# A decoder layer on one core: loop's end reordered, the last group's kept products added by GpSimd

## The reference

```python
x = _layernorm(x + attn(x, ...))                 # state-space block, 128 heads of 64, 8 groups
x = _layernorm(x + xattn(x, ctx, ctx, 0, mask))  # 32 query heads, 8 key heads of 16, context 128
x = _layernorm(x + ffn(x, W_gate, W_up, W_down)) # 1792 wide, silu(gate) * up
```

## Time and profile before

| | us |
|---|---|
| median of 3 runs (1641.96 to 1643.02) | 1642.07 |
| the profiled execution | 1646.22 |
| its span, first to last instruction | 1644.4 |

### The profile page before, as it was taken

One profiled execution on the slowest core, in us unless ns is written; L12 is line 12 of the kernel. 1 busy time (PEld: TensorE's weight loads), 2 busy tenths in 40 slices (PEclk: granted clock), 3 DMA queues, 4 the chain that ended last, 5 costly groups with the idle time before them and its releaser, 6 DMA issues.

```text
span 1644.4 us, 25600 instructions
## 1 busy us (share of the span) xinstructions
PE 1615.6 (98%) x9120; PEld 1274.3 (77%) x9120; DVE 1196.1 (73%) x2360; ACT 947.6 (58%) x1578; POOL 968.2 (59%) x736
## 2 busy tenths in 40 slices
PE   9999999999999999999999999999999998889998
PEld 7788888888888888888888888888888885445646
DVE  7767687767877786768686868586858688995433
ACT  6765377446745583648364837383728366994231
POOL 2977478656956694759484949495938563331000
PEclk9999999999999999999999999999999999999999
DMA  5432134212312241224131423141414173000000
GB/s 190 152 108 78 58 104 134 78 59 100 131 59 83 90 135 58 90 76 131 63 103 58 135 74 106 46 135 60 133 45 135 58 104 111 1 21 20 13 14 26
DMA packets 76547, 138.85 MB, mean 84 GB/s; under 512 B 6786, under 2 KB 13954, under 8 KB 76164
## 3 DMA queue, kind: packets, MB, share of 16 engines
q1 hardware_dynamic: 76420, 137.21, 26.3%
HBM read 134.55 MB, written 2.63 MB: 83 GB/s over the span
## 4 chain that ended last, share of the span: by engine, by line
PE 90%; DVE 7%; issue 1%; DMA 1%; ACT 0%; POOL 0%; SPq 0%; DVEq 0%; POOLq 0%; ACTq 0%
PE ps_hs L249 8%; PE ps_hs L251 8%; PE ps_hs L250 8%; PE ps_gate L250 7%; PE ps_gate L249 7%; PE ps_gate L251 7%; PE ps_y L1211 7%; PE ps_hs L1219 7%; PE ps_hs L1221 7%; PE ps_hs L1220 7%; PE ps_gate L1195 4%; PE ps_y L1503 3%; PE ps_hs L1465 3%; PE ps_dec L1465 3%; DVE pr L1043 2%; DVE conv L781 1%
## 5 line engine op out<-in xcount | busy, mean ns | idle before, releaser
L781 DVE SCALAR_TENSOR_TENSOR conv<-ps_hs,cw,conv 128x508 f32<-128x508 f32 (+2 forms) x432 | 320.2, 741 | 31.7 <-ACT conv L550 20.5
L395 POOL TENSOR_TENSOR cum_bc<-cum_bc,neg_cum 128x1024 f32<-128x1024 f32 x128 | 247.5, 1934 | 10.8 <-POOL cum_bc L385 0.3
L249 PE MATMUL ps_hs<-x_hi,w_hi 128*128 128x512 f32 x576 | 231.3, 402 | 0.0
L251 PE MATMUL ps_hs<-x_hi,w_lo 128*128 128x512 f32 x576 | 225.1, 391 | 0.0
L249 PE MATMUL ps_gate<-x_hi,w_hi 128*128 128x512 f32 x576 | 224.3, 389 | 0.0
L250 PE MATMUL ps_hs<-x_lo,w_hi 128*128 128x512 f32 x576 | 224.2, 389 | 0.0
L250 PE MATMUL ps_gate<-x_lo,w_hi 128*128 128x512 f32 x576 | 224.1, 389 | 0.0
L251 PE MATMUL ps_gate<-x_hi,w_lo 128*128 128x512 f32 x576 | 224.1, 389 | 0.0
L1219 PE MATMUL ps_hs<-wo_hi,g_hi 128*128 128x512 f32 x488 | 190.9, 391 | 0.0
L1221 PE MATMUL ps_hs<-wo_hi,g_lo 128*128 128x512 f32 x488 | 190.6, 390 | 0.0
L1220 PE MATMUL ps_hs<-wo_lo,g_hi 128*128 128x512 f32 x488 | 190.6, 390 | 0.0
(11 more groups left out here) (176 smaller groups left out, 3331.9 us busy)
## 6 DMA issues: line engine op xcount, KB each, us to landing
cum_bc<-cum_scratch SPq DMA_DIRECT2D x128, 512.0 KB, 4.1
w_raw<-w_in SPq DMA_DIRECT2D x145, 256.0 KB, 4.6
wo_raw<-w_out SPq DMA_DIRECT2D x64, 256.0 KB, 4.9
g_acc<-x_t SPq DMA_DIRECT2D x4, 512.0 KB, 6.2
acc<-x_nat SPq DMA_DIRECT2D x1, 2048.0 KB, 9.8
k_rep<-ctx_t SPq DMA_DIRECT2D x8, 256.0 KB, 12.9
out<-y_out SPq DMA_DIRECT2D x8, 256.0 KB, 2.0
wg_sb<-w_gate SPq DMA_DIRECT2D x1, 1792.0 KB, 15.7
```

The costliest lines, as they stand in the source:

```text
L249: eng.matmul(ps, whi, xhi, start=(k == 0), stop=False)
L251: return eng.matmul(ps, wlo, xhi, start=False, stop=(k == n - 1))
L395: gp.tensor_tensor(part, part, start.broadcast_to([P, 2, HB, SEQ]), ALU.add).then_inc(S["bc_ok"], 1)
L781: v.scalar_tensor_tensor(out=dst, in0=src, scalar=cw[:, at, TAPS - 1 - n:TAPS - n], in1=dst, op0=ALU.mult, op1=ALU.add).then_inc(S["tap"], 1)
```

## The change

- **Start.** Three passes over `dt`, the negation of `a_col` and the multiply by it go from VectorE to GpSimd, between `split(1)` and `split(2)`; ScalarE's L531 uses Relu instead of Identity. TensorE and SP wait for the new counts.
- **Loads.** `k_rep` is loaded from DRAM twice (to partitions 0 and 64 on); `v_raw` follows; SP waits for the two, and six DMAs copy them on inside SBUF.
- **Loop's end.** Kept products: ScalarE multiplies `g_acc` by `rstd_g` (`scale_kept`), GpSimd adds (`add_kept`), batches 0 to 4 after `k_bd` 1, 5 and 6 after 2, 7 after 3. VectorE's `second_part` waits for this; `first_part` is gone. Batch 0 alone is normed first. `LAST_PS` gives the batches other banks. TensorE does batches 0 to 2, turns the queries of batch 0, and does 3 to 7 among the first scores; VectorE's adds 3 to 7 stand in chunks 0 to 3.
- **Attention.** From batch 2 on, queries are turned into `ps_y[0]` (`Q_PS`), and ScalarE copies them ahead of its exponentials. `X2_STEPS` is two iterations earlier; `x2_high` stands ahead of the exponentials and `x2_low` between the two halves of the masked chunk. GpSimd's `powers` come in three parts (batch 1; 2 and 3; 4 to 7) and, for the second norm, at iteration 23 instead of 24.
- **Tail.** TensorE leaves its loop two iterations earlier and mixes the last turns and values with the first MLP tiles.

The diff, cut:

```diff
-X2_STEPS = (27, 29, 31, 33)
+X2_STEPS = (25, 27, 29, 31)
...
-        LAST_PS = ps_hs + ps_gate + ps_dec + ps_gate
+        LAST_PS = ps_hs + ps_dec + ps_gate + [ps_y[1], ps_y[0]]
...
+        Q_PS = (BACK_PS, BACK_PS, PV_PS)
...
-                for r in range(REP):
+                src = ctx_t.rearrange("b (c q d) t -> q d (b c) t", q=2, d=AD)[par]
+                sp.dma_start(k_rep[par * 64:par * 64 + AD, :, :, :].rearrange("p b c t -> p (b c) t"), src)\
+                    .then_inc(S["k_in"], 16)
+            sp.dma_start(v_raw[:, :, :], ctx_nat.rearrange("b t d -> t b d")).then_inc(S["v_in"], 16)
+            sp.wait_ge(S["k_in"], 16 * 2)
+            for par in range(2):
+                first = k_rep[par * 64:par * 64 + AD, :, :, :]
+                for r in range(1, REP):
                     p0 = par * 64 + r * AD
-                    src = ctx_t.rearrange("b (c q d) t -> q d (b c) t", q=2, d=AD)[par]
-                    sp.dma_start(k_rep[p0:p0 + AD, :, :, :].rearrange("p b c t -> p (b c) t"), src)\
-                        .then_inc(S["k_in"], 16)
-            sp.dma_start(v_raw[:, :, :], ctx_nat.rearrange("b t d -> t b d")).then_inc(S["v_in"], 16)
+                    sp.dma_start(k_rep[p0:p0 + AD, :, :, :], first).then_inc(S["k_in"], 16)
...
             split(1)
+            pool.wait_ge(S["a_exp"], 1)
+            gp.tensor_scalar(a_col[:, :], a_col[:, :], -1.0, None, ALU.mult).then_inc(S["dt_pool"], 1)
+            pool.wait_ge(S["dt_dve"], 2)
+            pool.wait_ge(S["dt_act"], 6)
+            gp.tensor_tensor(dt_l, dt_l, dt_u, ALU.subtract).then_inc(S["dt_pool"], 1)
+            pool.wait_ge(S["dt_pool"], 2)
+            gp.tensor_tensor(dt_v, dt_v, dt_l, ALU.add).then_inc(S["dt_pool"], 1)
+            pool.wait_ge(S["dt_pool"], 3)
+            gp.tensor_scalar(dt_v, dt_v, 100.0, 0.0, ALU.min, ALU.max).then_inc(S["dt_pool"], 1)
+            pool.wait_ge(S["dt_pool"], 4)
+            gp.tensor_tensor(dt_u, dt_v, a_col[:, 0:1].broadcast_to([P, TOK]), ALU.mult).then_inc(S["dt_pool"], 1)
...
-            def powers(stage, cols):
+            def add_kept(b):
+                pool.wait_ge(S["acc_ok"], BATCH * (GROUPS - 2) + b + 1)
+                pool.wait_ge(S["kept_sc"], b + 1)
+                gp.tensor_tensor(acc[:, b, :], acc[:, b, :], g_acc[:, b, :], ALU.add).then_inc(S["acc_ok"], 1)
...
+                if i == 1:
+                    for b in range(5):
+                        add_kept(b)
+                    powers(1, 0, slice(1, 2))
+                if i == 2:
+                    add_kept(5)
+                    add_kept(6)
                 if i == 3:
-                    powers(1, slice(2, HB))
-                if i == 7:
-                    powers(1, slice(HB, BATCH))
-                if i == 24:
-                    powers(2, slice(0, HB))
+                    add_kept(7)
+                if i == 3:
+                    powers(1, 1, slice(2, HB))
+                if i == 8:
+                    powers(1, 2, slice(HB, BATCH))
+                if i == 23:
+                    powers(2, 0, slice(0, HB))
...
-                sc.activation(dt_v[:, h * HALF:(h + 1) * HALF], ps_y[h][:, :], ACT.Identity, bias=dtb_col[:, :])\
+                sc.activation(dt_v[:, h * HALF:(h + 1) * HALF], ps_y[h][:, :], ACT.Relu, bias=dtb_col[:, :])\
...
-                sc.activation(q_t[b % 2][:, :, :].rearrange("p k s -> p (k s)"), BACK_PS[:, :], ACT.Copy,
+                sc.activation(q_t[b % 2][:, :, :].rearrange("p k s -> p (k s)"), Q_PS[min(b, 2)][:, :], ACT.Copy,
...
-            root(1, 0, slice(0, 2))
+            def scale_kept(b):
+                sc.activation(g_acc[:, b, :], g_acc[:, b, :], ACT.Copy, scale=rstd_g[:, b:b + 1])\
+                    .then_inc(S["kept_sc"], 1)
+            act.wait_ge(S["rstd_inv"], GROUPS)
+            act.wait_ge(S["gacc_ok"], BATCH * (2 * GROUPS - 1))
+            for b in range(3):
+                scale_kept(b)
+            root(1, 0, slice(0, 1))
+            sc.activation(rstd[2][:, 0:1], ones[:, 0:1], ACT.Exp).then_inc(S["exp_table"], 1)
             keep_queries(0)
-            sc.activation(rstd[2][:, 0:1], ones[:, 0:1], ACT.Exp).then_inc(S["exp_table"], 1)
+            for b in range(3, BATCH):
+                scale_kept(b)
             act.wait_ge(S["g_ok"], 2 * TILES)
             for i in range(1, CHUNKS + 3):
                 if 0 <= i - 3 < CHUNKS:
                     keep_turned(i - 3)
+                if i == 3:
+                    keep_queries(1)
+                if i % KD == 1 and 1 < i // KD + 1 < BATCH:
+                    keep_queries(i // KD + 1)
+                if i in X2_STEPS:
+                    x2_high(X2_STEPS.index(i), BACK_PS)
                 if i - 1 < CHUNKS:
                     exponentials(i - 1, 0)
-                if i % KD == 1 and i // KD + 1 < BATCH:
-                    keep_queries(i // KD + 1)
                 if i % 2 == 0 and i >= 6:
                     keep_values((i - 6) // 2)
                 if i - 1 < CHUNKS:
                     exponentials(i - 1, 1)
-                if i in X2_STEPS:
...
-            dve.wait_ge(S["dt_dve"], 2)
-            dve.wait_ge(S["dt_act"], 6)
-            v.tensor_tensor(dt_l, dt_l, dt_u, ALU.subtract).then_inc(S["dt_dve"], 1)
-            dve.wait_ge(S["dt_dve"], 3)
-            v.scalar_tensor_tensor(out=dt_v, in0=dt_v, scalar=0.0, in1=dt_l, op0=ALU.max, op1=ALU.add)\
-                .then_inc(S["dt_dve"], 1)
-            dve.wait_ge(S["dt_dve"], 4)
-            v.tensor_scalar(dt_v, dt_v, 100.0, 0.0, ALU.min, ALU.max).then_inc(S["dt_dve"], 1)
             taps(0, 0, 1)
             taps(0, 1, 0)
             taps(0, 1, 1)
-            dve.wait_ge(S["a_exp"], 1)
-            v.tensor_scalar(a_col[:, :], a_col[:, :], -1.0, None, ALU.mult).then_inc(S["dt_dve"], 1)
-            dve.wait_ge(S["dt_dve"], 6)
-            v.tensor_scalar(dt_u, dt_v, a_col[:, 0:1], None, ALU.mult).then_inc(S["dt_dve"], 1)
...
             dve.wait_ge(S["gacc_ok"], BATCH * (2 * GROUPS - 1))
             invert_group(GROUPS - 1)
-            for b in range(2):
-                first_part(b)
-                second_part(b)
-                first_stats(b)
-            variances(1, 0, first_two)
-            first_part(2)
+            second_part(0)
+            first_stats(0)
+            variances(1, 0, slice(0, 1))
+            inverses(1, 0, slice(0, 1))
+            normed(1, 0, acc[:, 0, :]).then_inc(S["x1_ok"], 1)
+            second_part(1)
             second_part(2)
-            inverses(1, 0, first_two)
-            normed(1, 0, acc[:, 0, :]).then_inc(S["x1_ok"], 1)
-            for b in range(3, 5):
-                first_part(b)
-                second_part(b)
-            normed(1, 1, acc[:, 1, :]).then_inc(S["x1_ok"], 1)
-            first_part(5)
-            second_part(5)
-            first_part(6)
-            first_part(7)
...
                     masked(i, 0)
-                    if i == 0:
-                        second_part(7)
+                    if i in X2_STEPS:
+                        x2_low(X2_STEPS.index(i), BACK_PS)
                     masked(i, 1)
-                if i + 2 < BATCH:
-                    first_stats(i + 2)
+                if i == 0:
+                    second_part(3)
+                    first_stats(1)
+                if i == 1:
+                    second_part(4)
+                    second_part(5)
+                    dve.wait_ge(S["pow1"], 1)
+                    normed(1, 1, acc[:, 1, :]).then_inc(S["x1_ok"], 1)
+                if i == 2:
+                    second_part(6)
+                    first_stats(2)
+                    first_stats(3)
+                if i == 3:
+                    second_part(7)
+                if 3 <= i < BATCH - 1:
+                    first_stats(i + 1)
                 if i % 2 == 0 and i >= 8:
                     n = (i - 8) // 2
...
-                    dve.wait_ge(S["pow1"], 1 + b // HB)
+                    dve.wait_ge(S["pow1"], 2 + b // HB)
                     normed(1, b, acc[:, b, :]).then_inc(S["x1_ok"], 1)
-                if i == 24:
+                if i == 23:
                     dve.wait_ge(S["pow2"], 1)
                 if i + 2 in X2_STEPS:
                     b = X2_STEPS.index(i + 2)
                     normed(2, b, acc[:, b, :]).then_inc(S["x2_ok"], 1)
-                if i in X2_STEPS:
-                    x2_low(X2_STEPS.index(i), BACK_PS)
             dve.wait_ge(S["kbd_ok"], CHUNKS)
...
+            last_products((4,), (0, 1))
             outputs(t, 0)
...
+            last_products((5,), (0, 1))
             outputs(t, 1)
...
+            pe.wait_ge(S["ss_part"], 1)
+            last_products((2,), range(TPH))
             pe.wait_ge(S["g_lo_ok"], 2 * t + 2)
-            pe.wait_ge(S["ss_part"], 1)
-            last_products((4, 5), range(TPH))
             def turn_queries(b):
...
-                    need(pe, S["q_sb"], b)
+                need(pe, S["q_sb"], b)
```

(47 more changed lines are left out.)

51 lines of the change are left out of this document (21 added, 30 removed).

## The result

| | us | | us |
|---|---|---|---|
| before, median of 6 | 1642.34 (1641.87 to 1644.38) | before, profiled execution | 1646.22, span 1644.4 |
| after, median of 6 | **1650.47** (1648.96 to 1652.45) | after, profiled execution | 1649.57, span 1647.7 |

The ratio after to before is 1.0036 (95% interval 1.0022 to 1.0050), some 6 us; the two medians lie 8.1 us apart, at the upper end of that interval. The forecast was 1642.8, its range ended at 1647.0, and it gave "slower" a chance of 0.22.

A forecast was written before the change was run, and what follows sets the result against it. TensorE was taken as full from 60 to 1340 us, with waits at the start and in the attention loop. Terms 2.6 - 8.6 + 3.5 + 1.8 = -0.7 us gave 1646.9 profiled, 1642.8 against the median; range 1631.5 to 1647.

The forecast's parts named there:

- part 3: Attention loop: query turns no longer wait for VectorE's attention result; 3.5 us gained, bounds 1 and 5.3.
- their cover: Attention loop: VectorE's 3.4 us a chunk was to cover GpSimd's power steps holding up k_bd; nothing counted.
- the sum: Whole kernel: 2.6 - 8.6 + 3.5 + 1.8 = -0.7 us, so 1646.9 profiled and 1642.8 against the median.
- Part 1, the start: Kernel start: passes moved from VectorE to GpSimd let the scan and causal step start earlier; 2.6 us gained, bounds 2.0 and 3.2.
- Part 2, the entry: Attention loop's entry: TensorE idles 8.5 us because the adds wait for k_rep's copies; -8.6 us, bounds +1.6 and -15.
- A: Entry, the forecast itself: copies move at 16 partitions' pace and TensorE's idle time eats the rest; 1638.5 to 1646.5, chance 0.50.
- B: Entry: copies run as fast as the weights, k_rep there by 1351 us; 1632.6 us, chance 0.28.
- C: Entry: copies of the two halves overlap in part, k_rep at 1358 us; 1637.6 us, chance 0.14.
- D: Entry: copies to partitions 32 and 96 take twice as long, k_rep at 1367.2 us; 1647.5 us, chance 0.08.
- the wait named: Attention loop: TensorE's query turns waiting for VectorE's attention result, 5.4 us in 5 places, were to stop waiting.
- the row's 5.3 us: Attention loop: ScalarE's waits for TensorE's turned probabilities, 5.3 us, taken as the upper bound of the loop's gain.
- Part 4, the tail: Attention's end: the MLP's first products start earlier, mixed with the last turns and values; 1.8 us gained, bounds 0 and 3.

The follow-up runs named there:

- e2: Kernel before with only the stage 2 power step moved from behind k_bd 24 to behind k_bd 23: ratio 1.0041 to the kernel before.
- e1: Changed kernel with the stage 2 power step of batches 0 to 3 back behind k_bd 24: ratio 1.0015 to the kernel before.
- e9: Kernel before with the start part alone (three passes and the multiply by GpSimd, Relu by ScalarE): ratio 0.9993 to the kernel before.
- e13: Kernel before with the start part, and GpSimd's next weight split waiting for VectorE's eight scans: ratio 0.9979 to the kernel before.
- e6: Changed kernel with k_rep filled by two copies of 16 partitions and two of 32, instead of six of 16: ratio 1.0017 to the kernel before.
- e12: Changed kernel with k_rep filled by two 64-partition loads from 64 consecutive DRAM rows, no copies: ratio 0.9965 to the kernel before.
- e8: Changed kernel with the query turns' wait for VectorE's attention result put back: ratio 1.0072 to the kernel before.
- e10: Changed kernel with the loop's last turns and values ahead of the MLP's first products again: ratio 1.0047 to the kernel before.
- e4: Changed kernel with k_rep filled by two 64-partition loads whose DRAM source repeats 16 rows four times, no copies: ratio 1.0164 to the kernel before.
- e14: Changed kernel with adds before k_rep's wait, power step split, two 16- and two 32-partition copies, weight split waiting for scans: 1632.76 us, ratio 0.9922 to the kernel before.

## Why the prediction was wrong

**The step that failed** is a sentence of part 3: "GpSimd's power steps hold up fewer k_bd; their cover is VectorE's 3.4 us a chunk, and I count nothing." One of them holds up k_bd 24 for longer than the cover: TensorE idles 4.5 us and comes back at half clock, 5.6 us in the trace, 6.7 alone (e2), 3.4 to 4.4 back when undone (e1). I counted how many k_bd stand behind power steps and not on what each step waits. The dependency could be read from the code: batch 3's statistics are made in VectorE's chunk 22, behind scores 22, and k_bd 24 may be made as soon as scores 22 are done; a step between k_bd 23 and 24 that needs these statistics takes away all of k_bd 24's lead.

A second step failed in the last line of the sum, "That one is 4.15 us above the median of 1642.07; against the median it is" 1642.8: by the medians it is worth 5.0 us, as much as the stall, by the ratio 2.6 (see "The sum" below).

Part 1, the start: **2.6 forecast, 2.2 in the pair of traces, 1.5 on average of twelve, 1.2 by e9's times.** GpSimd's passes were right to 0.8 us. But "the scan starts at 28.8 instead of 32.65 us" was followed by the round trip "at 39.0 instead of 42.58 us", which carried the scans' 2.63 us over to a place where GpSimd's weight split runs beside them; they took 5.55 (e13 shows it). I named the split only as something that is wanted late, not as something that disturbs.

Part 2, the entry: -8.6 forecast, **-7.8 measured**, by the way argued. k_bd 0 "starts near 1360 us": 1360.27. "Idle for some 8 us": 8.15. The copies kept the pace of 16 partitions: the first landed at 1347.8, the last at 1360.2, 2.5 us each for 2.36. This, and e6 and e12, bear A out, the forecast's own case; B, C and D fall. (D, at 1647.5, lay outside the range that was to reach it.)

Part 3, the loop: +3.5 forecast, +4.5 up to chunk 20, by the wait named (e8). The mechanism was right and the size 1 us too low: ScalarE was expected to keep 1.8 of the row's 5.3 us back, and 0.8 stayed away; no run shows whose those are.

Part 4, the tail: +1.8 forecast, +2.9 from n = 28. The MLP's first product starts at 1487.48 us, level with the earlier trace rows although chunk 31's copy is 6.6 us late, because it now stands ahead of the last turns; e10 shows 1.3 us of the gain as the order's. The forecast's bounds were "0 if the clock falls as it did, 3 if no wait is left"; the clock did not fall, and the upper bound came.

**The sum.** Without the stall these terms give a gain of 2.3 us where the forecast's sum gave a loss of 0.7: the profiled execution of after would take 1644.0. With it, it takes 1649.6, 2.7 above the forecast's 1646.9: 5.6 us of stall less 3.0 by which the other terms came out better, 1 us of it in the loop and 1.6 behind chunk 21. The forecast of the median is off by 7.7, so the other 5.0 us lie in the transfer: I took "4.15 us above the median" as a constant of the profile, and the changed kernel's profiled execution lies 0.9 below its median. The ratio, 6 us, puts this error at 2.6 us instead. The window behind the tile loop shows how executions differ, for the kernel before and then for e9:

```profile
1349.00:1359.00 10.00, 9.96 (x41) 8.20 (x42) 7.03 (x15) 2.58 (x4) 0.25 (x2) 0.66 1.26 119
```

```profile
1350.00:1356.00 6.00, 6.00 (x29) 5.03 (x29) 4.23 (x11) 1.08 (x2) 0.00 (x0) 0.73 1.28 97
```

In both, TensorE is busy throughout and its clock is at the 1.2 GHz level for a part, which costs 3.4 us before (0.34 of 10) and 1.6 in e9 (0.27 of 6). e2, built like the kernel before, has the short form too, and in both the slip is 1.6 us smaller at n = 0 than at the mask's load. So executions differ by some 1.7 us at this place. In the changed kernel the stretch costs nothing, since TensorE idles behind it anyway until the copies are there; this can be one reason why the times differ by more than the two traces. That the runs behind the median had the short stretch is not shown, and e13, whose trace has the long one (3.4 us), lies only 0.4 above its median. What the record does show is that the kernel before's own runs spread with their mean granted clock: beside e1 the fastest took 1641.40 us at 0.998 and the slowest 1648.59 at 0.994, and the profiled one, 1646.22, had 0.996. The rest I can't place.

## What to carry to other kernels

When an instruction is moved forward in an in-order queue, write down for each one behind it when its inputs are there and when its result is wanted; count waits, not instructions. An add that is ready must not stand behind a transfer that it doesn't need, and a step for several batches waits for the last of them, so it is split where only the first is wanted soon. Work handed from VectorE to GpSimd can be paid for by VectorE instructions with two SBUF inputs that then run beside GpSimd, even if both engines have time. And an absolute time worked out from one profiled execution inherits that execution's luck; here it was worth 5 us.

## What the runs showed of the hardware that I had not expected

- A scan on VectorE, which reads two SBUF tensors, lasted 2.54 us instead of 0.40 beside a 2.38 us GpSimd subtraction, and 1.2 beside a cast of 1.04; without them beside it, 0.40 again (e13). It looks held rather than slowed: it ended 0.3 us behind the subtraction, at 31.64 for 31.36 us, and the next scans ran at full speed. The Trainium skill, SBUF — State Buffer, section "Who interferes with whom", states this as an exclusive lock of the shared port pair; the trace agrees with 2.54 us for 2.38. By this rule the prediction could have priced the start.
- A DMA whose outermost source dimension is a repeat of 4 kept the DMA engines busy for a quarter of their time: 66 GB/s at a share of 0.25, against 213 at 0.99 (e4, e12).
- GpSimd's multiply of 1024 columns by one column took 1.90 us, its two-tensor forms 2.41.
- Behind the one-column square sums at the tile loop's end, TensorE's clock fell to the 1.2 GHz level while the engine stayed busy, and what that cost varied between executions: 3.4 us in the kernel before and in e13, 1.6 in e9, and nothing in e14, where the clock read 1.00 from 1330 to 1358 us.
- The same stop of 2.12 us near the attention's end was followed by a clock of 0.50 in the kernel before and in e9, and by 1.00 in e13.
